# Mixture of experts by pairs of experts, its first groups prepared inside attention

## The chip, the cores and the metric

One core of a Trainium2 chip runs the whole kernel in one launch. The metric is the device time in microseconds, the median of several runs. TensorE (PE) multiplies, VectorE (DVE), ScalarE (ACT) and GpSimd (POOL) do element work, SyncE (SP) issues transfers and transposes by DMA. Each engine works through its own list in order and waits on semaphores.

## The reference

A vision tower of one layer over 64 images of 3x224x224. Each image gives 196 patches of 768 numbers and a class token, so 197 tokens of 192 channels:

```
h = concat(cls, patches @ W_lin.T + b_lin)            # 64 x 197 x 192
h = h + attention(layernorm(h))                        # 12 heads of 16, q and k normalised
x = layernorm(h)
h = h + moe(x)
moe(x):  s = sigmoid(x @ gate.T)                       # 8 experts in 4 groups
         biased = s + bias; best 2 of 4 groups by sum; best 2 experts in them
         w = s[chosen] / (sum + 1e-6)
         y = sum_e w_e * (silu(x @ w1_e.T) * (x @ w3_e.T)) @ w2_e.T
         z = same with the shared expert's weights, weight 1
```

All experts are computed for all tokens; the weight of those not chosen is 0. fp32 operands are split into two fp16 parts (hi and lo), so that a product is made of several fp16 matmuls.

## The kernel before

**Phase A** (`phase_a`, one block) does patches and attention. Its steps run as a pipeline over `k = 0 .. 68`: in step k, image k is embedded, k-2 is projected to q, k and v, k-3 is scored, k-4 attended, k-5 projected, added to the residual and stored to `hidden_dram`. Every engine has its own `step(k)` with the order of its work written out by hand. After step 63 no new image enters and the steps empty out.

**Phase B** (`phase_b`, a second block, which starts when all engines have left the first) takes the 12608 tokens from `hidden_dram` in 25 groups: 24 of 512 tokens (4 to a partition) and a last one of 320. For each group: SP loads `hin` (L994), DVE takes statistics (`stats_of`, L1171), POOL makes scale and shift (`rstds`, L1320 to L1329), ACT normalises and rounds to fp16 (`normalise`, L1108 to L1117), POOL takes the rest (`rest_of`, L1344), SP turns both parts by eight DMA transposes (L1008, L1009), PE multiplies by the gate (`gate`, 20 small matmuls, L1040), ACT takes tanh (L1123), and DVE picks the experts in 19 small steps cut into parts 0 to 5 (`route`). This is done one or two groups ahead, except for group 0 (and the normalising of group 1), which nothing precedes.

Nine experts (the ninth is the shared one) are computed for each group. For expert e:

- PE `inner_products`: eight matmuls of 128 rows (L1054 to L1057), then two "tails" of 64 rows (L1061), which use the upper and the lower half of the array beside each other, into the banks `ps_h1[b]` and `ps_h3[b]`, b alternating.
- ACT `silu` (L1132), DVE `multiply` (L1252), ACT `inner_first` (in_hi, L1140), POOL `inner_rest` (in_lo, L1337).
- PE `outer_products` (twelve matmuls, L1075 to L1077) for the expert two before, into `ps_y[0]` and `ps_y[1]`.
- DVE `accumulate` (L1270, or L1276 for the shared expert).

PE's order is inner(e), outer(e-2), inner(e+1), outer(e-1) and so on. POOL's `inner_rest(e)` also waits for the silu of expert e+1 (L1335), so that it starts when DVE starts the next multiply. An inner(e) waits for the multiply of e-2, an outer for the accumulation of the expert before, half by half.

Of the kernel before, what the change touches and what calls it, by code (L numbers as in the profile page):

```python
# [16 lines left out]
F32 = mybir.dt.float32  # L17
# [14 lines left out]
C = 192  # L32
# [73 lines left out]
def vit_layer(nc, xp, w_lin, bias_cls, w_qkv, w_proj, w_gate, gate_bias, w13, w2,  # L106
              ident, before4, before8, out):
    hidden_dram = nc.dram_tensor("hidden_dram", [IMAGES, TOKENS, C], F32).ap()
    with ExitStack() as ctx:
# [7 lines left out]
        with ExitStack() as passing:  # L117
# [23 lines left out]

            lin_f = stage("lin_f", [128, PCHUNKS, C])
# [39 lines left out]
            phase_a(nc, xp, hidden_dram, sem, locals())  # L182
        phase_b(nc, hidden_dram, out, sem, sb, locals())


def phase_a(nc, xp, hidden_dram, sem, bufs):
# [17 lines left out]
    with ExitStack() as ctx:  # L204
# [57 lines left out]

        def run(step):

            for k in range(IMAGES + 5):
                step(Index(0, k))
# [5 lines left out]
        def _(sp):  # L272
# [45 lines left out]
        def _(pe):  # L318
# [186 lines left out]
            run(step)  # L505


        @block.scalar
        def _(act):
# [90 lines left out]
            def step(k):  # L600
# [34 lines left out]
                if 0 <= k.c - FIRST_PIECE < PIECES:  # L635
                    mixture_piece(k.c - FIRST_PIECE)

# [4 lines left out]
            run(step)  # L642


        @block.vector
        def _(dve):
# [158 lines left out]
            def step(k):  # L805
# [42 lines left out]
                if k.c == 0:  # L848
                    attention_weights()

# [8 lines left out]
        def _(pool):  # L859
# [29 lines left out]
            for k in range(3, IMAGES + 3):  # L889
# [3 lines left out]
                strips_of(Index(0, k - 3), 1)  # L893


def phase_b(nc, hidden_dram, out, sem, sb, bufs):

    w13_hi, w13_lo, w2_hi, w2_lo, gate_hi, gate_lo, gbias, bef4, bef8, minus_half = (
        bufs[n] for n in "w13_hi w13_lo w2_hi w2_lo gate_hi gate_lo gbias bef4 bef8 minus_half".split())
    with ExitStack() as ctx:
        def ps(name, shape, dt=F32):
            return ctx.enter_context(nc.psum_tensor(name, shape, dt))

        T, E, G = LANES, EXPERTS, EGROUPS
        hin = [sb(f"hin{p}", [128, T, C]) for p in range(3)]
        acc = [sb(f"acc{p}", [128, T, C]) for p in range(2)]
# [9 lines left out]
        yT_lo = [sb(f"yT_lo{p}", [128, 2, GT], F16) for p in range(3)]  # L919
        act1 = [sb(f"act1{p}", [INTER, GT]) for p in range(2)]  # L920
        inner = [sb(f"inner{p}", [INTER, GT]) for p in range(3)]
        in_hi = [sb(f"in_hi{p}", [INTER, GT], F16) for p in range(3)]
        in_lo = [sb(f"in_lo{p}", [INTER, GT], F16) for p in range(3)]
        half = sb("half", [128, T, E])
# [19 lines left out]
        ps_y = [ps(f"ps_y{b}", [128, 512]) for b in range(2)]  # L944
        ps_gate = ps("ps_gate", [128, 512])

        h_in = [sem(f"h_in{p}") for p in range(3)]
        yT_in = [sem(f"yT_in{p}") for p in range(3)]
        acc_out = [sem(f"acc_out{p}") for p in range(2)]

        gate_done, inner_done, y_done = sem("gate_done"), sem("inner_done"), sem("y_done")

        yhi_done, tanh_done, silu_done, inhi_done = (
            sem("yhi_done"), sem("tanh_done"), sem("silu_done"), sem("inhi_done"))

        bst_done, bmv_done, bnorm_done, ylo_done = (
            sem("bst_done"), sem("bmv_done"), sem("bnorm_done"), sem("ylo_done"))
        route_step, route_done = sem("route_step"), sem("route_done")
        mul_done, inlo_done, acc_done = sem("mul_done"), sem("inlo_done"), sem("acc_done")

        bve_done, brstd_done, bshift_done, bneg_done = (
            sem("bve_done"), sem("brstd_done"), sem("bshift_done"), sem("bneg_done"))

        tokens_in = hidden_dram.rearrange("n t c -> (n t) c")
        tokens_out = out.rearrange("n t c -> (n t) c")
        LAST = FULL
        GROUPS_B = FULL + 1

        def rows_of(g):
            return REST if g.known and g.i * 2 + g.c == LAST else 128  # L970

        def full(dram):
            return dram[0:FULL * GT].rearrange("(g p t) c -> g p t c", p=128, t=T)

        def part(dram, g):
            if rows_of(g) == 128:
                return full(dram)[g.times(1)]
            return dram[FULL * GT:TOTAL].rearrange("(p t) c -> p t c", t=T)
# [9 lines left out]
        def _(sp):  # L988
            def load(g):
                p = g.mod(3)  # L990

                if reached(g.times(2 * NE, 2 - 6 * NE)):
                    sp.wait_ge(acc_done, g.times(2 * NE, 2 - 6 * NE))
                sp.dma_start(hin[p][0:rows_of(g)], part(tokens_in, g)).then_inc(h_in[p], 16)  # L994

# [5 lines left out]
            def transposes(g, half_no):  # L1001
                R, p = rows_of(g), g.mod(3)
                sp.wait_ge(ylo_done, g.times(2, half_no + 1))
                if half_no == 0 and reached(g.times(NE, -2 * NE)):
                    sp.wait_ge(inner_done, g.times(NE, -2 * NE))
                for t in (2 * half_no, 2 * half_no + 1):
                    s = slice(t * R, (t + 1) * R)
                    sp.dma_start_transpose(yT_hi[p][:, :, s], y_hi[0:R, t, :]).then_inc(yT_in[p], 16)  # L1008
                    sp.dma_start_transpose(yT_lo[p][:, :, s], y_lo[0:R, t, :]).then_inc(yT_in[p], 16)  # L1009

            for g in range(3):
                load(Index(0, g, 2, GROUPS_B))
            for g in range(2):
                transposes(Index(0, g, 2, GROUPS_B), 0)
                transposes(Index(0, g, 2, GROUPS_B), 1)

            def body(g):
                ahead = g.back(-2)
                if g.back(-3).active():
                    load(g.back(-3))  # L1020
                if ahead.active():
                    transposes(ahead, 0)
                    transposes(ahead, 1)
# [6 lines left out]
        def _(pe):  # L1030
            def gate(g):
                R, p = rows_of(g), g.mod(3)
                pe.wait_ge(yT_in[p], 32 * T * (g.c // 3 + 1))

                if reached(g.times(1)):
                    pe.wait_ge(tanh_done, g.times(1))
                for t in range(T):
                    s = slice(t * R, (t + 1) * R)
                    dst = ps_gate[0:R, t * E:(t + 1) * E]
                    pe.matmul(dst, yT_hi[p][:, 0, s], gate_hi[:, 0], start=True, stop=False)  # L1040
                    pe.matmul(dst, yT_hi[p][:, 0, s], gate_lo[:, 0], start=False, stop=False)
                    pe.matmul(dst, yT_lo[p][:, 0, s], gate_hi[:, 0], start=False, stop=False)
                    pe.matmul(dst, yT_hi[p][:, 1, s], gate_hi[:, 1], start=False, stop=False)
                    last = pe.matmul(dst, yT_lo[p][:, 1, s], gate_lo[:, 1], start=False, stop=True)
                last.then_inc(gate_done, 1)

            def inner_products(g, e):
# [5 lines left out]
                for w, bank in enumerate(banks):  # L1053
# [3 lines left out]
                    pe.matmul(bank, w13_hi[:, 1, e, w, :], y_hi[:, 1], start=False, stop=False)  # L1057
                for w, bank in enumerate(banks):
# [5 lines left out]
            def outer_products(g, e):  # L1064
                R, b = rows_of(g), e % 3
# [351 lines left out]
```

## Time and profile before

| | us |
|---|---|
| median of 3 runs | 1692.89 (1692.03 to 1693.24) |
| the profiled execution, device time | 1693.34 |
| its span, first to last instruction | 1690.9 |
| PE busy in the span | 1602.8 (95%) |
| DVE, ACT, POOL busy | 1276.7, 989.0, 676.4 |
| mean granted TensorE clock, share of full | 0.985 |

The profiled execution is 0.45 us above the median. PE's busy time is made of modelled spans of overlapping matmuls, so start-to-start distances in the timeline say more than durations.

### The profile page before, as it was taken

How to read it: one execution, taken by the hardware profiler on the slowest of the kernel's cores; microseconds unless marked ns; L12 is line 12 of the kernel's file. 1: busy time of each engine (PE TensorE's matmuls, PEld its weight loads, DVE VectorE, ACT ScalarE, POOL GpSimd, SP SyncE). 2: the span in 40 equal slices, each digit the busy share in tenths (PEclk: the TensorE clock that was granted, in tenths of full speed). 3: DMA queues.
4: the chain of work that ended last, by engine and by line, in shares of the span. 5: the costliest groups of instructions: out<-in, count | busy, mean ns of one | idle time of the engine just before them, and what ended most of it. 6: DMA issues, size and time to landing. Idle time of an engine off the chain costs nothing. (4 is left out here: it accounts for less than half of the span.)

```text
span 1690.9 us, 44146 instructions
## 1 busy us (share of the span) xinstructions
PE 1602.8 (95%) x16714; PEld 1098.8 (65%) x16714; DVE 1276.7 (76%) x3610; ACT 989.0 (58%) x2039; POOL 676.4 (40%) x758
## 2 busy tenths in 40 slices
PE   4999999999999999999998299999999999999998
PEld 4777777777777777777776155555555555555555
DVE  5777877777777777777774288888887888888877
ACT  2777777667777777777676245454545454444543
POOL 2333333333333333333331255454554545454543
PEclk8999999999999999999999599999999999999999
DMA  7233333333333333333310211212121111112110
GB/s 245 64 78 78 77 77 78 77 78 78 80 79 79 79 82 80 78 81 78 77 27 12 56 47 37 59 34 61 33 58 38 45 51 43 53 40 56 34 36 16
DMA packets 97695, 108.11 MB, mean 64 GB/s; under 512 B 61323, under 2 KB 74286, under 8 KB 97358
## 3 DMA queue, kind: packets, MB, share of 16 engines
q1 hardware_dynamic: 88270, 85.83, 17.6%
q0 software_dynamic: 9216, 19.47, 7.6%
q8 instruction: 134, 2.20, 0.5%
q14 instruction: 75, 0.61, 0.1%
HBM read 92.44 MB, written 19.37 MB: 66 GB/s over the span
## 5 line engine op out<-in xcount | busy, mean ns | idle before, releaser
L1337 POOL TENSOR_TENSOR in_lo<-inner,in_hi 128x512 f16<-128x512 f32 (+1 forms) x225 | 259.7, 1154 | 347.8 <-ACT act L1132 335.4
L884 POOL CAST qk_strips<-qk_norm 99x768 f16<-99x768 f32 x128 | 105.2, 822 | 583.1 <-DVE qk_norm L753 583.1
L589 ACT ACTIVATE prob<-ps_sc 99x792 f32<-99x792 f32 x384 | 303.8, 828 | 6.2 <-PE ps_sc L404 2.6
L1140 ACT ACTIVATE in_hi<-inner 128x512 f16<-128x512 f32 (+1 forms) x225 | 140.3, 623 | 203.5 <-DVE inner L1252 203.5
L1270 DVE SCALAR_TENSOR_TENSOR acc<-ps_y,comb,acc 128x192 f32<-128x192 f32 (+1 forms) x700 | 242.0, 408 | 0.3 <-PE ps_y L1077 0.3
L1132 ACT ACTIVATE act<-ps_h 128x512 f32<-128x512 f32 (+1 forms) x225 | 131.9, 586 | 168.4 <-PE ps_h L1061 168.4
L1252 DVE SCALAR_TENSOR_TENSOR inner<-ps_h,act 128x512 f32<-128x512 f32 (+1 forms) x225 | 153.0, 680 | 102.3 <-ACT act L1132 99.9
L1075 PE MATMUL ps_y<-w_hi,in_hi 128*128 128x192 f16 (+1 forms) x900 | 224.2, 249 | 4.0 <-DVE acc L1270 3.4
L1077 PE MATMUL ps_y<-w_hi,in_lo 128*128 128x192 f16 (+1 forms) x900 | 221.4, 246 | 0.0
L1076 PE MATMUL ps_y<-w_lo,in_hi 128*128 128x192 f16 (+1 forms) x900 | 221.4, 246 | 0.0
L342 PE MATMUL ps_hid<-lin_hi,x_hi 128*99 128x192 f16 x768 | 193.9, 252 | 19.1 <-DVE x_lo L701 10.4
L344 PE MATMUL ps_hid<-lin_hi,x_lo 128*99 128x192 f16 x768 | 190.9, 249 | 0.0
L343 PE MATMUL ps_hid<-lin_lo,x_hi 128*99 128x192 f16 x768 | 190.9, 249 | 0.0
L1054 PE MATMUL ps_h<-yT_hi,w_hi 128*128 128x512 f16 (+1 forms) x450 | 169.5, 377 | 1.9 <-DVE inner L1252 1.9
L886 POOL TENSOR_TENSOR qk_strips<-qk_norm,qk_strips 99x384 f16<-99x384 f32 x128 | 165.9, 1296 | 10.6
L419 PE MATMUL ps_o<-prob,v 98*32 98x198 f32 (+1 forms) x3072 | 169.8, 338 | 0.0
L1057 PE MATMUL ps_h<-yT_hi,w_hi 128*128 128x512 f16 (+1 forms) x450 | 169.6, 377 | 0.0
L1056 PE MATMUL ps_h<-yT_hi,w_lo 128*128 128x512 f16 (+1 forms) x450 | 169.6, 377 | 0.0
L1055 PE MATMUL ps_h<-yT_lo,w_hi 128*128 128x512 f16 (+1 forms) x450 | 169.6, 377 | 0.0
L764 DVE COPY kT<-ps_mix 128x594 f16<-128x594 f16 x128 | 60.5, 473 | 96.9 <-PE ps_mix L388 96.2
L571 ACT ACTIVATE qT<-ps_mix 128x594 f16<-128x594 f16 x128 | 86.8, 678 | 66.8 <-PE ps_mix L388 66.8
L404 PE MATMUL ps_sc<-qT,kT 64*99 64x198 f16 x1536 | 105.8, 256 | 21.1 <-ACT prob L589 19.9
(157 smaller groups left out, 3807.3 us busy)
## 6 DMA issues: line engine op xcount, KB each, us to landing
xin<-xp SPq DMA_DIRECT2D x64, 594.0 KB, 4.3
x_hi<-xp POOLq DMA_DIRECT2D x64, 297.0 KB, 4.1
hidden_dram<-h SPq DMA_DIRECT2D x64, 147.0 KB
hin<-hidden_dram SPq DMA_DIRECT2D x24, 384.0 KB, 3.5
out<-acc SPq DMA_DIRECT2D x24, 384.0 KB, 2.7
w_f<-w SPq DMA_DIRECT2D x1, 2304.0 KB, 9.1
yT_hi<-y_hi SPq DMA_TRANSPOSE x100, 2.4
yT_lo<-y_lo SPq DMA_TRANSPOSE x100, 2.4
```

Source lines behind the costliest of these rows:

```text
L342: pe.matmul(hid[:, t, :], hi[:, k, s], lin_hi[:, k, :], start=(k == 0), stop=False)
L343: pe.matmul(hid[:, t, :], hi[:, k, s], lin_lo[:, k, :], start=False, stop=False)
L344: last = pe.matmul(hid[:, t, :], lo[:, k, s], lin_hi[:, k, :], start=False, stop=(k == PCHUNKS - 1))
L419: last = pe.matmul(o_quad[VB * place:VB * place + VB, :], v[p][rows, m, QUAD * quad + place, :], prob[quad][rows, place, m, :], start=(m = ...
L589: act.activation(prob[quad][:, places].rearrange("p h m s -> p h (m s)"), ps_sc[0:TR, places, 0:2 * SLOTS], ACT.Exp, scale=D ** -0.5 / (SQ ...
L1055: pe.matmul(bank, w13_hi[:, 0, e, w, :], y_lo[:, 0], start=False, stop=False)
L1056: pe.matmul(bank, w13_lo[:, 0, e, w, :], y_hi[:, 0], start=False, stop=False)
L1075: pe.matmul(dst, in_hi[b][:, s], w2_hi[:, e, :], start=True, stop=False)
L1076: pe.matmul(dst, in_hi[b][:, s], w2_lo[:, e, :], start=False, stop=False)
L1077: last = pe.matmul(dst, in_lo[b][:, s], w2_hi[:, e, :], start=False, stop=True)
L1270: last = dve.scalar_tensor_tensor(out=acc[p][0:R, t, :], in0=ps_y[half_no][0:R, u * C:(u + 1) * C], scalar=comb[p][0:R, t, e:e + 1], in1=b ...
L1337: pool.tensor_tensor(in_lo[b][:, 0:N], inner[b][:, 0:N], in_hi[b][:, 0:N], ALU.subtract).then_inc(inlo_done, 1)
```

## The change

Two edits. First, the objects for preparing a group's rows move out of `phase_b` into a class `MixtureRows` that lives through both phases, and phase A's steps call it. SP loads groups 0 to 2 in step 58. DVE takes group 0's statistics at the end of steps 61 and 62 and group 1's at the end of steps 66 and 67. POOL makes group 0's scale and shift after its step 63. ACT normalises group 0 at the end of steps 64 and 65, POOL takes the rest in steps 65 and 66, SP issues four transposes in each of its steps 65 and 66 after the store. ACT loads the table for silu at the end of step 67. After its last step PE multiplies group 0 by the gate (into the unused end of `ps_hid`), ACT normalises group 1 and takes group 0's tanh, and POOL makes group 1's scale, shift and rest. Group 1's eight transposes are SP's first work in phase B.

Second, experts are done two at a time over the whole run of 225 (group, expert) pairs. The buffers `inner`, `in_hi`, `in_lo` go from 3 to 4, `ps_y` from 2 banks to 4 (a pair for each parity of the expert); the gate's scores go to the end of one of them. POOL's wait for the next silu is gone.

```
+                if k.c == IMAGES - 6:                      # SP, phase A
+                    for p in range(2):
+                        sp.wait_ge(h2_out[p], 32 * 4)
+                    for g in range(3):
+                        rows.load(sp, b_group(g))
+                if k.c in (IMAGES + 1, IMAGES + 2):
+                    rows.transposes(sp, b_group(0), k.c - IMAGES - 1)
             run(step)                                      # PE, phase A
+            pe.wait_ge(v_set, IMAGES)
+            rows.gate(pe, b_group(0), ps_gate)
+                if k.c in (IMAGES, IMAGES + 1):            # ACT, phase A
+                    rows.normalise(act, b_group(0), k.c - IMAGES)
+                if k.c == IMAGES + 3:
+                    act.preload_act_table_set("silu_and_others")
             run(step)
+            rows.normalise(act, b_group(1), 0)
+            rows.normalise(act, b_group(1), 1)
+            rows.gate_out(act, b_group(0), ps_gate)
+                if k.c in (IMAGES - 3, IMAGES - 2):        # DVE, phase A
+                    rows.stats_of(dve, b_group(0), k.c - IMAGES + 3)
+                if k.c in (IMAGES + 2, IMAGES + 3):
+                    if k.c == IMAGES + 2:
+                        dve.wait_ge(rows.bneg_done, 1)
+                    rows.stats_of(dve, b_group(1), k.c - IMAGES - 2)
+                if k == IMAGES - 1:                        # POOL, phase A
+                    rows.rstds(pool, b_group(0))
+                if k in (IMAGES + 1, IMAGES + 2):
+                    rows.rest_of(pool, b_group(0), k - IMAGES - 1)
+            rows.rstds(pool, b_group(1))
+            rows.rest_of(pool, b_group(1), 0)
+            rows.rest_of(pool, b_group(1), 1)
...
+        def two_by_two(own_work, older_work):              # phase B
+            turns = [(Index(0, g, 2, GROUPS_B), e) for g in range(GROUPS_B) for e in range(NE)]
+            for i in range(0, len(turns) + 2, 2):
+                own, older = turns[i:i + 2], turns[max(i - 2, 0):i]
+                own_work(own, lambda: [older_work(g, e) for g, e in older])
...
             def outer_products(g, e):
-                R, b = rows_of(g), e % 3
+                if g.c == 0 and e == 0:
+                    pe.wait_ge(tanh_done, 1)
+                R, b, y = rows_of(g), (NE * g.c + e) % 4, ps_y[(g.c + e) % 2]
...
-                    if reached(g.times(2 * NE, 2 * e + half_no - 1)):
-                        pe.wait_ge(acc_done, g.times(2 * NE, 2 * e + half_no - 1))
+                    if reached(g.times(2 * NE, 2 * e + half_no - 3)):
+                        pe.wait_ge(acc_done, g.times(2 * NE, 2 * e + half_no - 3))
...
+            def turn(own, older_products):                 # PE
+                for g, e in own:
                     inner_products(g, e)
+                scored = [g.back(-1) for g, e in own if e == 3 and g.back(-1).active()]
+                for following in scored:
+                    g, e = own[0]
+                    if reached(g.times(2 * NE, 2 * e - 6)):
+                        pe.wait_ge(acc_done, g.times(2 * NE, 2 * e - 6))
+                    rows.gate(pe, following, ps_gate)
+                for g, e in own:
+                    inner_tails(g, e)
+                for following in scored:
+                    pe.wait_ge(tanh_done, following.times(1, 1))
+                older_products()
+            two_by_two(turn, outer_products)
...
+            def turn(own, _):                              # ACT
+                for g, e in own:
+                    if e == 3 and g.back(-1).active():
+                        if g.c == 0:
+                            act.wait_ge(route_step, 1)
+                        rows.gate_out(act, g.back(-1), ps_gate)
+                for g, e in own:
                     silu(g, e)
+                for g, e in own:
                     inner_first(g, e)
+                for g, e in own:
+                    ahead = g.back(-2)
+                    if e == 5 and ahead.active():
+                        rows.normalise(act, ahead, 0)
+                    if e == 6 + g.c % 2 and ahead.active():
+                        rows.normalise(act, ahead, 1)
...
+            def turn(own, older_sums):                     # DVE
+                for g, e in own:
                     multiply(g, e)
+                older_sums()
+                for g, e in own:
+                    following, ahead = g.back(-1), g.back(-2)
+                    if g.c == 0 and e == 0:
+                        for part_no in range(5):
+                            route(g, part_no)
+                    if e == 0:
+                        route(g, 5)
                     if e in (1, 2) and ahead.active():
+                        rows.stats_of(dve, ahead, e - 1)
+                    if e > 3 and following.active():
                         route(following, e - 4)
...
             def inner_rest(g, e):                          # POOL
                 pool.wait_ge(inhi_done, g.times(NE, e + 1))
-                if e + 1 < NE or g.back(-1).active():
-                    pool.wait_ge(silu_done, g.times(NE, e + 2))
...
                     if e == 3 and g.back(-2).active():
+                        rows.rstds(pool, g.back(-2))
+                    if e == 6 and g.back(-2).active():
+                        rows.rest_of(pool, g.back(-2), 0)
+                    if e == 7 + g.c % 2 and g.back(-2).active():
+                        rows.rest_of(pool, g.back(-2), 1)
```

`inner_tails` is the second half of the old `inner_products` (the two matmuls of 64 rows), unchanged; the methods of `MixtureRows` are the old local functions with the engine as an argument.

## Rows read from the trace of the kernel before

**Rows 1.** Stretches: busy us (instructions) by engine, TensorE clock, DMA share, GB/s.
```profile
937.00:963.50 26.50, 0.51 (x19) 0.51 (x20) 3.66 (x17) 4.76 (x12) 5.96 (x12) 0.50 0.25 71
1000.00:1640.00 640.00, 639.08 (x4828) 366.18 (x4827) 533.36 (x1617) 311.78 (x597) 326.96 (x375) 1.00 0.18 46
```

**Rows 2.** Waits of PE from 970 us on: us in total, times, longest.
```profile
PE ps_y L1075 <- DVE acc L1270: 3.4, 6, 1.1
```

**Rows 3.** Timeline between the phases: start, us, engine, line, operation, idle before it.
```profile
936.86 0.56 DVE L802 SCALAR_TENSOR_TENSOR h<-ps_mix,h 99x384 f32<-99x384 f32 x1 [1.99 <-PE ps_mix L325]
...
940.31 1.29 SPq L994 DMA_DIRECT2D hin<-hidden_dram  x3
...
948.37 0.98 ACT L1108 ACTIVATE bnorm<-hin,bshift,brstd 128x192 f32<-128x192 f32 x2 [14.11 <-POOL bshift L1329]
...
950.01 0.97 ACT L1108 ACTIVATE bnorm<-hin,bshift,brstd 128x192 f32<-128x192 f32 x2
...
951.51 1.29 SPq L1008 DMA_TRANSPOSE yT_hi<-y_hi  x1
...
960.56 1.25 SPq L1009 DMA_TRANSPOSE yT_lo<-y_lo  x1
...
962.99 0.19 PE L1040 MATMUL ps_gate<-gate_hi,yT_hi 128*128 128x8 f16 x1 [26.17 <-DMA yT_lo<-y_lo]
...
963.55 0.59 PE L1054 MATMUL ps_h<-yT_hi,w_hi 128*128 128x512 f16 x1
```

**Rows 4.** Timeline of PE in the mixture, one expert's worth.
```profile
1302.98 0.38 PE L1054 MATMUL ps_h<-yT_hi,w_hi 128*128 128x512 f16 x1
...
1304.49 0.38 PE L1057 MATMUL ps_h<-yT_hi,w_hi 128*128 128x512 f16 x1
...
1304.80 0.39 PE L1061 MATMUL ps_h<-yT_lo,w_lo 64*128 64x512 f16 x2
...
1305.13 0.26 PE L1075 MATMUL ps_y<-w_hi,in_hi 128*128 128x192 f16 x1
...
1306.13 0.38 PE L1054 MATMUL ps_h<-yT_hi,w_hi 128*128 128x512 f16 x1
```

**Rows 5.** Timeline of group 0: route parts 2 and 3, multiply, next inner.
```profile
968.74 0.17 DVE L1223 TENSOR_SCALAR chosen<-rank 128x16 f32<-128x16 f32 x1
...
970.86 0.69 DVE L1252 SCALAR_TENSOR_TENSOR inner<-ps_h,act 128x512 f32<-128x512 f32 x1
...
971.61 0.39 PE L1054 MATMUL ps_h<-yT_hi,w_hi 128*128 128x512 f16 x1 [1.86 <-DVE inner L1252]
```

**Rows 6.** Timeline of PE in attention: four successive couples of 64-row matmuls.
```profile
797.52 0.55 PE L404 MATMUL ps_sc<-qT,kT 64*99 64x198 f16 x8
...
797.82 0.25 PE L404 MATMUL ps_sc<-qT,kT 64*99 64x198 f16 x2
```

**Rows 7.** The tanh's line (duration ns min/median/max, first and last start).
```profile
L1123 ACT ACTIVATE half<-ps_gate x25: 175/178/198, 966.7 to 1644.4; 128x32 f32<-128x32 f32 x24, 80x32 f32<-80x32 f32 x1
```

**Rows 8.** Timeline of the mixture, what follows the tails that start at 1301.66.
```profile
1302.09 0.60 ACT L1132 ACTIVATE act<-ps_h 128x512 f32<-128x512 f32 x1 [1.16 <-PE ps_h L1061]
...
1302.78 0.69 DVE L1252 SCALAR_TENSOR_TENSOR inner<-ps_h,act 128x512 f32<-128x512 f32 x1 [0.69 <-ACT act L1132]
...
1303.39 1.38 DVE L1270 SCALAR_TENSOR_TENSOR acc<-ps_y,comb,acc 128x192 f32<-128x192 f32 x4
...
1303.51 0.63 ACT L1140 ACTIVATE in_hi<-inner 128x512 f16<-128x512 f32 x1 [0.82 <-DVE inner L1252]
```

**Rows 9.** One line of part 3 (duration ns min/median/max).
```profile
L1198 DVE TENSOR_TENSOR cmp<-masked x23: 411/615/919, 1025.0 to 1661.5; 128x256 f32<-128x256 f32 x22, 80x256 f32<-80x256 f32 x1
```

**Rows 10.** Timeline of POOL and DVE at 1575 us.
```profile
1575.32 1.16 POOL L1337 TENSOR_TENSOR in_lo<-inner,in_hi 128x512 f16<-128x512 f32 x1 [0.25 <-issue]
...
1575.38 1.37 DVE L1200 TENSOR_TENSOR eq<-eq,bef 128x256 f32<-128x256 f32 x1
```

**Rows 11.** Timeline of POOL, a rest of the rows ahead.
```profile
1573.58 0.92 POOL L1344 TENSOR_TENSOR y_lo<-bnorm,y_hi 128x384 f16<-128x384 f32 x1
```

More of the change, by code:

```diff
@@ new lines, in gate_out @@
+        def gate_out(act, g, bank):
+            R = rows_of(g)
+            act.wait_ge(gate_done, g.times(1, 1))
+            act.activation(half[0:R], bank[0:R, 0:T * E].rearrange("p (t e) -> p t e", e=E), ACT.Tanh,
+                           scale=0.5 / SS).then_inc(tanh_done, 1)
+        self.hin = hin
+        self.y_hi = y_hi
+        self.y_lo = y_lo
+        self.yT_hi = yT_hi
+        self.yT_lo = yT_lo
+        self.yT_in = yT_in
+        self.inner_done = inner_done
+        self.acc_done = acc_done
@@ new lines, in __init__, with phase_b, ps @@
+        self.bneg_done = bneg_done
+        self.rows_of = rows_of
+        self.part = part
+        self.tokens_out = tokens_out
+        self.GROUPS_B = GROUPS_B
+        self.half, self.gate_done, self.tanh_done = half, gate_done, tanh_done
+        self.gate, self.gate_out = gate, gate_out
+        self.load = load
+        self.transposes = transposes
+        self.normalise = normalise
+        self.stats_of = stats_of
+        self.rstds = rstds
+        self.rest_of = rest_of
+def phase_b(nc, out, sem, sb, rows, bufs):
+    w13_hi, w13_lo, w2_hi, w2_lo, gate_hi, gate_lo, gbias, bef4, bef8, minus_half = (
+        bufs[n] for n in "w13_hi w13_lo w2_hi w2_lo gate_hi gate_lo gbias bef4 bef8 minus_half".split())
+    hin, y_hi, y_lo, yT_hi, yT_lo, yT_in, inner_done, acc_done, rows_of, part, tokens_out, GROUPS_B = (
+        rows.hin, rows.y_hi, rows.y_lo, rows.yT_hi, rows.yT_lo, rows.yT_in, rows.inner_done, rows.acc_done, rows.rows_of, rows.part, rows.tokens_out, rows.GROUPS_B)
+    with ExitStack() as ctx:
+        def ps(name, shape, dt=F32):
+            return ctx.enter_context(nc.psum_tensor(name, shape, dt))
+        T, E, G = LANES, EXPERTS, EGROUPS
+        acc = [sb(f"acc{p}", [128, T, C]) for p in range(2)]
@@ L920, in phase_b @@
         act1 = [sb(f"act1{p}", [INTER, GT]) for p in range(2)]
[L921 to L924, printed above, removed]
+        inner = [sb(f"inner{p}", [INTER, GT]) for p in range(4)]
+        in_hi = [sb(f"in_hi{p}", [INTER, GT], F16) for p in range(4)]
+        in_lo = [sb(f"in_lo{p}", [INTER, GT], F16) for p in range(4)]
@@ L999, in store @@
                 sp.dma_start(part(tokens_out, g), acc[p][0:rows_of(g)]).then_inc(acc_out[p], 16)
[L1001 to L1015, printed above, removed]
+            second = Index(0, 1, 2, GROUPS_B)
+            rows.transposes(sp, second, 0)
+            rows.transposes(sp, second, 1)
             def body(g):
@@ L1019, in body @@
                 if g.back(-3).active():
-                    load(g.back(-3))
+                    rows.load(sp, g.back(-3))
                 if ahead.active():
-                    transposes(ahead, 0)
-                    transposes(ahead, 1)
+                    rows.transposes(sp, ahead, 0)
+                    rows.transposes(sp, ahead, 1)
                 store(g)
@@ L1030, in _ @@
         def _(pe):
[L1031 to L1045, printed above, removed]
             def inner_products(g, e):
```

300 lines of the change are left out of this document (131 added, 169 removed).

## The prediction, made blind

> **What bounds the kernel now.** I read the busy times by stretches first. In the mixture, from 1000 to 1640 us, PE is busy 639.1 of 640 us at full clock and DVE 533.4 [rows 1]; in the stretch from 937 to 963.5 us PE does 0.5 us of work in 26.5 and its clock is granted at 0.50, the lower of its two levels (1.2 GHz) [rows 1]. So there are two places to gain: the gap between the phases, and PE's own time in the mixture, where only work or lost slots of PE count. The waits confirm it: from 970 us to the end PE waits 3.4 us for DVE's sums, in six places [rows 2], and for little else.
>
> The timeline shows what the gap is made of [rows 3]: the last residual ends at 937.4, the first load is issued at 940.31 (store landed, engines in the new block), group 0's normalising can start at 948.37, its eight transposes go out from 951.51 to 960.56, one per 1.29 us, the last lands 2.43 us after its issue, and PE starts at 962.99 with the gate (0.56 us) and at 963.55 with the experts.
>
> One expert on PE takes 1306.13 - 1302.98 = 3.15 us [rows 4]. Eight full matmuls start 1.51/7 = 0.215 us apart. The tails start 0.31 after the last of them, and the first outer matmul 0.33 after the tails; at the pace of 512 columns each would be 0.215. So 0.095 + 0.11 = 0.205 us are lost around each couple of tails. The twelve outer matmuls take 1.00.
>
> **The change part by part.**
>
> *The gap.* Loading, statistics, scale and shift, normalising, eight transposes and gate of group 0 leave the gap. What they displace in attention: DVE's statistics (four short instructions a half, 1.2 us by the 0.30 an instruction below) fall at the ends of steps in which its loads shrink; I count nothing. ACT's normalise takes 950.01 - 948.37 = 1.64 us a half [rows 3] and stands in front of step 65's and step 66's exponents and copies, which the shortened steps wait for one after another. Bounds 0 and 3.3 us; I take 2, since the first stands before the copy that projection waits for and the second meets some slack. SP's eight transposes take its queue for 4 x 1.29 = 5.2 us twice, behind stores 60 and 61; images follow each other some 14 us apart (68 steps to 937), so the next store waits for nothing. The first tanh's table load is hidden in step 67, where ACT idles. So attention ends at 939.4, and the new block starts 2.9 us behind it as now (940.31 - 937.4), at 942.3. Behind this hides group 1's chain: ACT's last copy lies some 3 us before the last residual's end (a correction, the projection and the residual are between), at 936.4; two halves of 1.64 go to 939.7, the tanh to 940.2, POOL's last rest (two operations, 0.92 [rows 11] and, with a third of the columns, some 0.4, an estimate) to 941.2. They end about with the store; I set PE's first expert at 943.0. It is 962.99 now: **-20.0**. Group 0's gate, 0.56, is done beside ACT: **-0.5**.
>
> *The start of the mixture.* Now, at 971.61 PE starts its third expert [rows 5], having done 0.56 + 2 x 3.15 - 2 x 1.00 = 4.9 us of work in 8.6: 3.7 lost. After: half clock at first loses some 2 (both); nothing older covers the first silu and multiply, 1.3; group 1's eight transposes start only at 943 and land at 943 + 9.05 + 2.43 = 954.5, where PE asks for them at about 954, 0.7; DVE does route parts 0 to 5 between the second and the third multiply, 22 instructions at 2.12/7 = 0.30 [rows 5], 6.7 us, and a half of statistics: 1.2. Together 5.2: **+1.5**. At nought to +4.
>
> *Pairs on PE.* 112 times two experts: one stay of tails instead of two. Saved 0.205 each, if the second couple of tails follows the first at 0.215. The nearest rows: four couples of 64-row matmuls in attention start within 0.30 us, 0.10 apart for 198 columns [rows 6], which is 0.08 of streaming. So loading the next 64-row weights hides under the running ones but for 0.02. Bounds per pair: 0.205 and 0.10 (no hiding, one 0.10 load each); I take 0.20: 112 x 0.20 = **-22.4**.
>
> *Four banks of ps_y.* DVE's sums may now be a turn late; the 3.4 us of rows 2 go, but the tail of the run keeps some: **-2**.
>
> *The gate turns.* PE now waits for the tanh between tails and outer products. Gate matmuls, then 0.65 us of tails; tanh takes 0.18 [rows 7], with hand-overs 0.45. Hidden: 0. The 25 tanh share the table with silu today (one load each at the start only), so no reloads.
>
> *The new tight place.* Let a pair's tails start at 0. Now tails at 1301.66 (one period before 1304.80) are followed by silu at +0.43, multiply at +1.12 [rows 8], and PE can use the bank 971.61 - 970.86 = 0.75 after a multiply starts [rows 5]: +1.87. With pairs PE asks for it after the second tails (0.215), the change back (0.325) and 24 outer matmuls (1.98), at +2.52. So DVE may come 0.65 us late to a pair's first multiply; beyond that PE stands. Before, it asked a whole expert later. The turn is 2 x 3.15 - 0.2 = 6.1 us, DVE's work in it two multiplies (0.61 each, 1303.39 - 1302.78) and two sums (1.38 each less an overlap of 0.08 with what follows), which is 3.8, and routing or statistics. Parts 2 and 3 together take 970.86 - 968.74 = 2.1 us [rows 5], the largest load: 5.9, under 6.1. So DVE alone is never late.
>
> But DVE and POOL hold each other up. The compare of part 3 takes 0.41 alone and up to 0.92, median 0.62 [rows 9]; at 1575.38 the next operation of that size takes 1.37 beside POOL's in_lo of 1575.32 and ends 0.3 after it [rows 10]. Sums and multiplies (one operand in PSUM) take their usual time beside in_lo [rows 8]. With in_hi at +1.85 for 0.63 [rows 8] and the wait for the next silu gone, the two in_lo of a pair (1.16 each) run from about +2.7 to +4.9, beside the sums: free. The rests of the rows ahead (0.92 and some 0.4) come where routing is. In even groups experts 6 and 7 share a turn: POOL does in_lo, rest, in_lo, rest without a break from +2.7 to +7.4; DVE comes at +4.9 with parts 2 and 3, is held 0.8 behind in_lo, 0.9 and 0.4 behind the rest, and ends at +9.0 instead of +7.0. The next multiply was due at +7.2: 1.8 late, PE stands 1.2. In odd groups the rests fall after both in_lo in the turns (5,6) and (7,8), beside parts 1 to 4: by the same count 0.3 and 1.0. Upper bound 12 x 1.2 + 11 x 1.3 = 29; lower bound 0, if POOL and DVE slip past each other. I take the first in full and a third of the second: **+19**.
>
> A rule speaks here. The Trainium skill, page "SBUF — State Buffer", section "SBUF: two separate sides", says that DVE operations with two SBUF inputs and GpSimd operations exclude each other for a whole instruction, whoever starts first. By it alone each meeting costs the rest of POOL's instruction, and the sum would take the upper bound, 29; by the median of the compare a meeting costs 0.2, five of them 1.0 a turn, and almost nothing would reach PE. The trace agrees with the rule in its maxima (0.92, 1.37).
>
> **Sum**, against the profiled 1693.34: -20.0 - 0.5 + 1.5 - 22.4 - 2 + 19 = -24.4, so 1668.9; the median of the runs is 0.45 lower: **1668**.
>
> **The rivals.**
>
> *A. The contention stays hidden* (0.35). DVE and POOL miss each other, or ACT's normalise pushes the rest later, past the routing. For it: DVE has 5.4 us of work a turn on average (533.4 us in 100 turns' time), so lateness is made good at once. Against: POOL's work in turn (6,7) has no break. Then -43: 1649.
>
> *B. Weights of the second tails are not loaded beside the first* (0.07). Each pair saves 0.10 only: 11 us less, 1679. The couples in attention speak against it.
>
> *C. The handover gains little* (0.05). Something at phase A's end (group 1's rest, DVE behind transposes) holds the block's end some 12 us: 1680. Against: the estimate of every chain ends by 941.3.
>
> *D. Slower: DVE bound* (0.04). If DVE is held in every turn as in turn (6,7), by 2.0 us, a turn lasts 5.4 + 2.0 = 7.4 instead of the 6.3 of today: 112 x 1.1 = 123 more, less the 19 of the gap: 1797. It decides from 1.05 us of holding per turn on (5.4 + 1.05 = 6.3 + 19/112). Against it: rests fall in two or three turns of nine, and in the others POOL is done by +4.9.
>
> *The forecast, part of the contention shows*, has 0.49. Its own range is 1657 to 1681.
>
> The range for 8 in 10: from just under A with its uncertainties (a shorter gap, 1645) to above B and C, 1684. A difference under 0.2% (3.4 us) can't be told from none: faster needs less than 1689.5. All of forecast, A, B and C are faster, less a tail of the forecast: 0.93 faster, 0.03 same, 0.04 slower.
>
> **What would show it.** PE's first expert starts near 943 instead of 963.55, its clock low for some 4 us. One pair of experts takes 6.1 us between first inner matmuls, with one stretch of four tails, the second couple 0.21 to 0.23 after the first. The table of waits shows PE's first full matmul of a pair (L1054 now) waiting for DVE's multiply (some 1 to 1.3 us, once or twice in two groups) and hardly for its sums; those waits follow turns with experts 6 and 7 (5 and 6, 7 and 8), where DVE's compares run to 0.9 us and more. If that wait is missing, A holds. If the distance of the couples is over 0.3, B. If PE starts after 950, C. If a turn lasts over 6.3 on average, D, and I am wrong in sign.

## The result, and the profile after

The changed kernel takes **1680.75 us** (median of 3, 1680.17 to 1683.59) against 1692.89: 0.9934 times the time before, 95% interval 0.9915 to 0.9954. The profiled execution has a span of 1678.2 us against 1690.9. So it is faster by 12.1 us, a little under half of the forecast 24.9 (1692.89 to 1668), and inside the range. The sign held, and PE does stand for late multiplies as forecast; several terms of the sum had the wrong size.

The stretches of the changed kernel, columns as in [rows 1]:

```profile
937.00:963.50 26.50, 15.16 (x113) 8.03 (x111) 10.08 (x30) 6.00 (x14) 4.86 (x6) 0.74 0.12 26
1000.00:1640.00 640.00, 618.92 (x4796) 366.17 (x4795) 565.32 (x1598) 303.69 (x594) 319.50 (x374) 1.00 0.17 45
```

PE works 15.2 us in the gap's 26.5, where it did 0.5 [rows 1]. But in the mixture, where it was busy for 639.1 of 640 us, it is now busy for 618.9: 20 us of standing are new. PE's waits from 970 us on name what it stands for (us in total, times, longest):

```profile
PE ps_h L1191 <- DVE inner L1357: 19.7, 25, 1.0
PE ps_y L1056 <- issue: 2.8, 11, 0.5
PE ps_y L1219 <- POOL in_lo L1411: 0.4, 1, 0.4
```

The waits for sums of [rows 2] are gone. In their place PE waits 25 times for DVE's multiply before a pair's first matmul, and 11 times before the gate (the view puts these down to "issue"; what they are is read further below).

Counted from the starts of PE's matmuls, a turn of two experts takes 6.08 us bare (two single ones took 2 x 3.143), and the nine turns of two groups take on average 6.94, 6.98, 6.08, 6.08, 7.19, 6.09, 6.59, 6.08 and 6.19, beginning with experts (0,1) of the even group. The gate's 0.5 is in the second and the seventh. So PE loses 0.86 before turn (2,3), 1.11 after turn (8,0), 0.11 after the odd group's turn (7,8), and 0.42 in the even group's gate turn. DVE does a turn's multiplies first and its routing last, so each of these losses is the lateness left by the routing one turn earlier: 0.86 by the odd group's turn (7,8), 1.11 by turn (6,7), 0.11 by turn (5,6).

The totals by stage, in the profiled execution of each kernel (us; the same count; "rest" runs from the first expert of the last group to the end of the span):

| kernel | last residual starts | first expert | first two groups | two groups, mean of the next 22 | rest |
|---|---|---|---|---|---|
| before | 936.86 | 963.55 | 59.90 | 57.85 | 31.1 |
| changed | 938.38 | 946.33 | 63.29 | 58.21 | 28.2 |
| rows' part alone (x1) | 942.92 | 950.88 | 57.80 | 57.78 | 31.1 |
| pairs alone (x2) | 936.90 | 963.15 | 62.10 | 58.30 | 28.2 |
| remainders beside the multiplies (x3) | 940.40 | 948.36 | 61.85 | 55.72 | 28.2 |
| rows earlier (x4) | 940.72 | 943.98 | 62.28 | 58.23 | 28.2 |
| routing first (x6) | 938.24 | 946.19 | 58.73 | 58.18 | 28.2 |
| x3, x4 (earlier still) and x6 (x9) | 937.19 | 940.46 | 57.81 | 55.69 | 28.2 |

Where the mixture loses, the timeline of POOL and DVE in an even group's turn (6,7) shows (start, us, engine, line, operation):

```profile
1036.87 0.91 POOL L1043 TENSOR_TENSOR y_lo<-bnorm,y_hi 128x384 f16<-128x384 f32 x1
1037.75 0.42 POOL L1044 TENSOR_TENSOR y_lo<-bnorm,y_hi 128x128 f16<-128x128 f32 x1
1038.13 1.15 POOL L1411 TENSOR_TENSOR in_lo<-inner,in_hi 128x512 f16<-128x512 f32 x1
1038.15 1.16 DVE L1328 TENSOR_SCALAR chosen<-rank 128x16 f32<-128x16 f32 x1
1039.25 0.91 POOL L1043 TENSOR_TENSOR y_lo<-bnorm,y_hi 128x384 f16<-128x384 f32 x1
1039.35 0.84 DVE L1330 TENSOR_SCALAR drop<-chosen 128x16 f32<-128x16 f32 x1
1040.12 0.42 POOL L1044 TENSOR_TENSOR y_lo<-bnorm,y_hi 128x128 f16<-128x128 f32 x1
1040.22 0.37 DVE L1334 TENSOR_TENSOR masked<-biased,chosen 128x32 f32<-128x32 f32 x1
...
1042.10 1.29 DVE L1357 SCALAR_TENSOR_TENSOR inner<-ps_h,act 128x512 f32<-128x512 f32 x2
```

Read the ends: chosen ends at 1039.31, POOL's in_lo at 1039.28; drop at 1040.19, POOL's first subtraction at 1040.16; masked at 1040.59, the second at 1040.54. Each DVE instruction, of 0.17 to 0.19 us by itself, lasts until POOL's is over, three times in a row, 1.8 us in all. The multiply starts at 1042.10, and PE, due at 1041.7, starts at 1042.85.

### The profile page after: what moved, and what is told of

Its sections match the earlier page's. It is cut to its first block and busy times, and to the rows that moved or that the text cites. A ratio compares the mean times of both kernels' runs of the same rounds, so it can differ in the third digit from the quotient of the medians.

```text
span 1678.2 us, 44142 instructions
## 1 busy us (share of the span) xinstructions
PE 1586.3 (95%) x16714; PEld 1102.9 (66%) x16714; DVE 1315.0 (78%) x3610; ACT 978.6 (58%) x2038; POOL 669.8 (40%) x758
## 5 line engine op out<-in xcount | busy, mean ns | idle before, releaser
L1411 POOL TENSOR_TENSOR in_lo<-inner,in_hi 128x512 f16<-128x512 f32 (+1 forms) x225 | 253.6, 1144 | 353.6 <-ACT in_hi L1258 353.5
L1250 ACT ACTIVATE act<-ps_h 128x512 f32<-128x512 f32 (+1 forms) x225 | 120.7, 588 | 224.8 <-PE ps_h L1203 221.7
L1191 PE MATMUL ps_h<-yT_hi,w_hi 128*128 128x512 f16 (+1 forms) x450 | 170.7, 379 | 31.1 <-DVE inner L1357 23.6
L1357 DVE SCALAR_TENSOR_TENSOR inner<-ps_h,act 128x512 f32<-128x512 f32 (+1 forms) x225 | 143.1, 678 | 71.3 <-ACT act L1250 53.8
L1258 ACT ACTIVATE in_hi<-inner 128x512 f16<-128x512 f32 (+1 forms) x225 | 136.5, 624 | 91.8 <-DVE inner L1357 91.8
```

The source lines that it names most:

```text
L1191: pe.matmul(bank, w13_hi[:, 0, e, w, :], y_hi[:, 0], start=True, stop=False)
L1411: pool.tensor_tensor(in_lo[b][:, 0:N], inner[b][:, 0:N], in_hi[b][:, 0:N], ALU.subtract).then_inc(inlo_done, 1)
```

## The experiments

**The two parts, each alone.** x1 keeps the rows' part and takes back the order of before; x2 keeps the pairs and takes back the rows' part.

```diff
-        ps_y = [[ps(f"ps_y{b}{half_no}", [128, 512]) for half_no in range(2)] for b in range(2)]
-        ps_gate = ps_y[0][1][:, 2 * C:512]
+        ps_y = [ps(f"ps_y{b}", [128, 512]) for b in range(2)]
+        ps_gate = ps("ps_gate", [128, 512])
...
-            two_by_two(turn, outer_products)
+            run(body)
...
```

Every engine's loop of the mixture is that of before again. x2, at the mixture's start and likewise on each engine:

```diff
-                if k.c in (IMAGES, IMAGES + 1):
-                    rows.normalise(act, b_group(0), k.c - IMAGES)
...
+            for c in range(2):
+                rows.normalise(act, Index(0, c, 2, GROUPS_B), 0)
+                rows.normalise(act, Index(0, c, 2, GROUPS_B), 1)
```

> The rows' part alone: the first two groups' rows are prepared in the last steps of attention as in the changed kernel, but the mixture keeps the order of before, one expert after the other, with three inner buffers and two ps_y banks. Theory (the earlier start is all that the change has won, and the pairs lose a little): TensorE's first expert starts at about 946, as after the change, two groups of the mixture take 57.9 us as before, and the whole takes 1674 to 1678, some 4 us less than the changed kernel. Rival (the pairs win too, and the earlier start is given back in the mixture's first turns): two groups again take 57.9 us, but the time is 1681 or more.

x1: 1675.39 us, ratio 0.9902 (0.9888 to 0.9915), faster than the change as a whole, with 57.8 us for two groups. Its first expert started at 950.88, not at about 946: attention itself ended 4.5 us later in the profiled execution, though its code is that of the changed kernel (more on this at the end of the next section).

> The pairs alone: the mixture's order of the changed kernel, the rows prepared after attention as before. Theory (each turn saves 0.2 us on TensorE, and the turns' stalls take more than that back): two groups take 58.2 us against 57.87 of before, and the whole 1692 to 1697, no faster than before. Rival (the pairs by themselves are worth their 22 us and only collide with the handover's work): 1670 to 1676, two groups in 56 us.

x2: 1696.21 us, ratio 1.0022 (1.0013 to 1.0031), two groups in 58.3. So all the gain is the rows' part, and the pairs, as placed, cost about 4 us by themselves and 5 beside the rows' part. Counted from the first expert on they cost 7.3 there ((63.29 - 57.80) + 11 x (58.21 - 57.78) + 28.2 - 31.1); part of it hides in x1's later end of attention. The rivals fall.

**What the stalls of the pairs are.**

```diff
                 for e in range(NE):
+                    if e in (6 - g.c % 2, 8 - g.c % 2) and g.back(-2).active():
+                        pool.wait_ge(silu_done, g.times(NE, e + 1))
+                        rows.rest_of(pool, g.back(-2), int(e > 6))
                     inner_rest(g, e)
-                    if e == 3 and g.back(-2).active():
+                    if e == 3 - g.c % 2 and g.back(-2).active():
                         rows.rstds(pool, g.back(-2))
-                    if e == 6 and g.back(-2).active():
-                        rows.rest_of(pool, g.back(-2), 0)
-                    if e == 7 + g.c % 2 and g.back(-2).active():
-                        rows.rest_of(pool, g.back(-2), 1)
...
-                    if e == 6 + g.c % 2 and ahead.active():
+                    if e == 6 - g.c % 2 and ahead.active():
                         rows.normalise(act, ahead, 1)
```

(The first half's normalising likewise: e == 5 - g.c % 2.)

> The changed kernel with one thing placed otherwise: GpSimd's remainders of the rows (y_lo) wait for the next turn's first silu, so that they run beside VectorE's two multiplies, which read PSUM, and not beside its routing; in odd groups the normalising and the remainders come a turn earlier, so that their transposes land before the gate. Theory 1 (GpSimd's remainders hold VectorE's routing instructions, whose lateness stalls TensorE 0.85 and 1.1 us in two of nine turns, and the odd groups' transposes land 0.3 us late for the gate): the chosen and drop instructions fall from 1.16 and 0.84 us to under 0.3, both stalls fall under 0.4 us, two groups take 56.0 to 56.8 us against 58.22, the whole 1657 to 1665. Rival (these two turns simply hold too much VectorE work, with or without GpSimd beside it): the holds go, the stalls stay near 0.7 and 0.9, two groups take 57.7 or more, the whole 1674 or more.

x3: **1654.41 us**, ratio 0.9774 (0.9760 to 0.9787), 26 us under the changed kernel. Its rows: PE's waits, the stretch of [rows 1], the two held lines (ns min/median/max) and one turn; ahead of them the two held lines of the changed kernel:

```profile
L1328 DVE TENSOR_SCALAR chosen<-rank x21: 166/176/1166, 1038.2 to 1620.4; 128x16 f32<-128x16 f32 x21
L1330 DVE TENSOR_SCALAR drop<-chosen x21: 174/835/1007, 1039.3 to 1620.6; 128x16 f32<-128x16 f32 x21
```

```profile
PE ps_h L1191 <- DVE inner L1357: 0.6, 2, 0.4
...
1000.00:1640.00 640.00, 639.43 (x5026) 387.14 (x5026) 552.18 (x1670) 311.76 (x611) 326.87 (x381) 1.00 0.17 45
...
L1328 DVE TENSOR_SCALAR chosen<-rank x22: 161/168/174, 1037.5 to 1620.7; 128x16 f32<-128x16 f32 x21, 80x16 f32<-80x16 f32 x1
L1330 DVE TENSOR_SCALAR drop<-chosen x22: 171/174/175, 1037.7 to 1620.9; 128x16 f32<-128x16 f32 x21, 80x16 f32<-80x16 f32 x1
...
1039.65 0.91 POOL L1043 TENSOR_TENSOR y_lo<-bnorm,y_hi 128x384 f16<-128x384 f32 x1 [2.26 <-ACT act L1250]
1039.67 1.29 DVE L1357 SCALAR_TENSOR_TENSOR inner<-ps_h,act 128x512 f32<-128x512 f32 x2
1040.52 0.42 POOL L1044 TENSOR_TENSOR y_lo<-bnorm,y_hi 128x128 f16<-128x128 f32 x1
```

The same subtractions run beside two multiplies, which read one operand from PSUM and keep their 1.29 us. DVE does the same routing in the same turns, and PE waits 0.6 us in all instead of 19.7. So the rival, too much DVE work in these turns, falls. The stalls were the holds. All nine turns are bare but for the gate, 55.72 us for two groups, less than I had expected (56.0 to 56.8), and so is the whole (1657 to 1665 expected). One reservation: x3 also moves the odd groups' rows a turn earlier, so by itself it does not part the holds from the late transposes. In even groups only the place of the remainders changed, and the 1.11 after turn (8,0) is gone. The gate turn, where the odd groups' transposes count, went from 6.98 to 6.56, so 11 x 0.42 = 4.6 of the 26 us are theirs. The next rows show that wait.

In the changed kernel the odd groups' last remainder ends at 1014.12, the last transpose goes out at 1017.93, and the gate stands until it has landed, at 1020.27:

```profile
1013.51 0.61 POOL L1044 TENSOR_TENSOR y_lo<-bnorm,y_hi 128x128 f16<-128x128 f32 x1
...
1017.93 1.25 SPq L991 DMA_TRANSPOSE yT_lo<-y_lo  x1
...
1020.37 0.17 PE L1056 MATMUL ps_y<-gate_hi,yT_hi 128*128 128x8 f16 x1 [0.18 <-issue]
```

The view puts only 0.18 of it down, to "issue". The PE queue's own record of this wait, for the transposes and for the tanh of the group before, runs from 1017.17 to 1020.31, and the matmul before it would have let the gate start at 1020.02.

**What holds the handover.** Each engine's list for a block ends in an instruction DRAIN, called its closing drain here. The blocks' end in the changed kernel:

```profile
939.32 0.29 SPq L293 DMA_DIRECT2D hidden_dram<-h  x1
939.44 0.91 POOL L1043 TENSOR_TENSOR y_lo<-bnorm,y_hi 128x384 f16<-128x384 f32 x1 [0.33 <-ACT y_hi L1010]
940.31 0.43 POOL L1044 TENSOR_TENSOR y_lo<-bnorm,y_hi 128x128 f16<-128x128 f32 x1
946.30 1.17 SPq L990 DMA_TRANSPOSE yT_hi<-y_hi  x1
...
946.33 0.59 PE L1191 MATMUL ps_h<-yT_hi,w_hi 128*128 128x512 f16 x1 [7.47 <-PEq L206]
```

Nothing computes or moves from 941.4 to 946.3. The trace's record of GpSimd's closing drain runs from 939.41 to 946.05, 5.3 us past its last subtraction (940.73), while SP had closed at 941.43. Before, that drain lay at 911.8 to 918.1, hidden. x4 moves the rows' work three attention steps earlier:

```diff
-                if k.c in (IMAGES, IMAGES + 1):
-                    rows.normalise(act, b_group(0), k.c - IMAGES)
+                if k.c in (IMAGES - 3, IMAGES - 2):
+                    rows.normalise(act, b_group(0), k.c - IMAGES + 3)
+                if k.c in (IMAGES, IMAGES + 1):
+                    rows.normalise(act, b_group(1), k.c - IMAGES)
...
-            rows.normalise(act, b_group(1), 0)
-            rows.normalise(act, b_group(1), 1)
```

Loads, statistics, remainders and transposes of both groups go with it.

> The changed kernel with the rows' work three steps of attention earlier, and group 1's transposes inside attention too, so that GpSimd's last instruction of attention ends near 915 instead of 940.7. Theory (the mixture's first expert waits for GpSimd's closing drain, which ends 5 to 6 us after its last instruction, 946.05 in the changed kernel; without it the last store decides): first expert at 940.5 to 942.5, the whole 3 to 5 us less than the changed kernel, 1676 to 1678. Rival 1 (the handover is bound by something else of the same length, such as the last store or the fetch of the new code): first expert stays at 945 to 947, 1680 to 1682. Rival 2 (the work taken into full steps of attention delays each of them): attention's last residual comes 2 to 5 us later than 938.4, and the gain is gone.

x4: 1676.99 us, ratio 0.9906 (0.9892 to 0.9920). First expert 3.26 us behind the last residual's start instead of 7.95. GpSimd's last instruction ended at 919.63, not near 915, and its drain at 924.95, still out of the way. Rows of x4:

```profile
941.65 0.29 SPq L293 DMA_DIRECT2D hidden_dram<-h  x1
...
943.98 0.58 PE L1188 MATMUL ps_h<-yT_hi,w_hi 128*128 128x512 f16 x1 [2.78 <-PEq L206]
```

The expert did not start at 940.5 to 942.5, since the residual itself came 2.3 us later, as rival 2 had it; most of that is one step at a lower clock (below). The time's interval overlaps that of the changed kernel (0.9915 to 0.9954), so what x4 shows is in the trace, not in the 3.8 us of the medians. x4 moves much else; x5 touches the drain alone, it is the kernel before with one instruction more:

```diff
+            pool.wait_ge(h2_done, IMAGES)
+            pool.memset(eps[:], EPS)
```

> The kernel before with one instruction more: GpSimd clears one column ([128 x 1]) once attention's last residual is done, and has nothing else to do there. Theory (GpSimd's closing drain ends 5 to 6 us after its last instruction, whatever that is, and the mixture's block waits for it): the drain that ended at 918.1 in the kernel before ends at 943 to 944, SyncE's first load of the mixture goes out at 943.2 to 944.3 instead of 940.31, and the whole takes 1695 to 1697. Rival (the 5.3 us behind the last instruction came from what GpSimd had to do there, two long subtractions, or overlapped something else): the first load stays within 0.7 us of 940.31 and the time at 1692 to 1693.5.

x5: 1696.08 us (one run, before 1692.75). Its rows:

```profile
938.00 0.10 POOL L895 MEMSET eps<- 128x1 f32 x1 [24.73 <-DVE h L802]
938.31 0.29 SPq L286 DMA_DIRECT2D hidden_dram<-h  x1
943.64 1.29 SPq L996 DMA_DIRECT2D hin<-hidden_dram  x3
```

The first load goes out at 943.64, not 940.31 [rows 3]; the drain ends at 943.39, again 5.3 us behind a 0.1 us instruction. Of the 3.3 us, 0.5 are the residual's own (937.38 against 936.86). The theory holds. What makes the drain so long is open: the mixture's own takes 0.9. x10 tried one cause:

```diff
+            pool.dma_start(scratch[:], tokens_in[0:128]).then_inc(scratch_in, 16)
+            pool.wait_ge(scratch_in, 16)
```

> The kernel before with one DMA more that GpSimd issues and waits for at the start of the mixture, 128 rows of 768 B into a tile that nothing reads. In the kernel before GpSimd issues 64 DMAs in attention and none in the mixture, and its closing drain ends 5.3 us after its last instruction in the one and at most 0.9 us in the other. Theory (the drain is long in a stretch of the program in which GpSimd has issued a DMA): the mixture's closing drain grows from 0.88 us to some 5 us or more. Rival (its length has to do with attention's other work or with the new code behind it): it stays at 0.9 us. The time hardly tells them apart: 1692 to 1697 in both, since the last store ends 7 us after GpSimd's last instruction.

The mixture's drain takes 0.97 us, as the rival has it: one early DMA of GpSimd does not make it long. (1690.95 us, one run.)

**The first turns.**

```diff
-                    if g.c == 0 and e == 0:
-                        for part_no in range(5):
-                            route(g, part_no)
...
+            for part_no in range(5):
+                route(Index(0, 0, 2, GROUPS_B), part_no)
```

> The changed kernel with group 0's routing (parts 0 to 4) at the start of VectorE's mixture work, where it idles until the first silu, instead of behind the first two multiplies. Theory (TensorE's waits of 1.2 and 2.7 us before the second and third turns come from VectorE being late, the third's from this routing): the third turn starts 2.3 to 3 us after 963.65 less, that is at 960.7 to 961.5, and the whole takes 1676.5 to 1679. Rival (the first turns are held by the low clock and by the transposes of group 1, which land at 957.3, so that a wait that goes is replaced by another): the third turn at 963 or later, 1680 to 1682.

x6: 1675.12 us, ratio 0.9903 (0.9887 to 0.9920). The third turn starts 3.0 us earlier and without a wait (first row the changed kernel, second x6), and the turn after it loses nothing either, where it had lost 1.7: 4.6 us in the first two groups. The time is 1.4 us under what I expected, since only the third turn's wait was counted.

```profile
963.65 0.39 PE L1191 MATMUL ps_h<-yT_hi,w_hi 128*128 128x512 f16 x1 [2.69 <-DVE inner L1357]
```

```profile
960.64 0.38 PE L1191 MATMUL ps_h<-yT_hi,w_hi 128*128 128x512 f16 x1
```

**All of it.** x9 joins x3 and x6 and moves the rows a further three steps forward, so that none of their work is left in attention's last, shortened steps.

```diff
-                if k.c == IMAGES - 6:
+                if k.c == IMAGES - 12:
                     for p in range(2):
                         sp.wait_ge(h2_out[p], 32 * 4)
...
-                if k.c in (IMAGES, IMAGES + 1):
-                    rows.normalise(act, b_group(0), k.c - IMAGES)
+                if k.c in (IMAGES - 6, IMAGES - 5):
+                    rows.normalise(act, b_group(0), k.c - IMAGES + 6)
+                if k.c in (IMAGES - 3, IMAGES - 2):
+                    rows.normalise(act, b_group(1), k.c - IMAGES + 3)
```

> All remedies together: GpSimd's remainders beside the multiplies, group 0's routing first, and both groups' rows and transposes done in full steps of attention, six and more steps before its end, so that nothing of them is left in the last, shortened steps. Theory (the costs found are separate and add): attention's last residual at 937 to 938.5, first expert 3.3 us later at 940.3 to 941.8, first turns 3 us shorter, two groups in 55.7 us, the whole 1640 to 1646. Rival 1 (the last steps of attention still lose 2 to 4 us to a lower granted clock, with or without the rows' work in them): last residual at 940 or later, 1645 to 1650. Rival 2 (the first turns' waits turn into others): 1648 to 1653.

x9: **1641.02 us** (1640.65 to 1641.10), ratio 0.9696 (0.9682 to 0.9710), with attention's end, the first expert and two groups where the theory has them. The first two groups are 5.5 us shorter than in the changed kernel instead of 3 (63.29 to 57.81).

```profile
940.46 0.59 PE L1188 MATMUL ps_h<-yT_hi,w_hi 128*128 128x512 f16 x1 [2.79 <-PEq L206]
...
1000.00:1620.00 620.00, 619.58 (x4869) 374.40 (x4868) 535.15 (x1621) 302.90 (x592) 316.91 (x369) 1.00 0.17 46
```

## Why the prediction was wrong

In the prediction's own terms (us; measured from the starts of PE's matmuls, twelve pairs of groups):

| term | predicted | measured |
|---|---|---|
| gap and gate | -20.5 | 946.33 - 963.55 = -17.2 |
| start of the mixture | +1.5 | (63.29 - 58.21) - (59.90 - 57.85) = +3.0 |
| pairs | -22.4 | 12 x 9 x (6.287 - 6.077) = -22.7, and 0.9 in the last group = -23.6 |
| four banks | -2 | 12 x 0.26, and 2.0 in the last group = -5 |
| gate turns | 0 | 12 x 0.42 = +5 |
| contention | +19 | 12 x (1.11 + 0.86 + 0.11) = +25 |
| sum | -24.4 | -13 (the two profiled spans differ by 12.8) |

- *The pairs on PE* came out as counted: what is lost around the tails is paid once instead of twice, and the second couple of tails starts 0.226 us after the first (median of 113), so loading its weights costs next to nothing. Rival B is out.
- *The four banks* gave 3 us more than counted: of PE's waits for DVE's sums, 2.8 us lay in the last group, and none is left. That it made up for part of the misses below is luck.
- *The contention* is the largest miss, and the step that failed is "a third of the second". Turn (6,7) was counted at 1.2 and costs 1.11. The odd groups' turns were counted at 0.3 and 1.0 and cost 0.11 and 0.86, nearly the full count. The prediction gives no reason for the third; the low price that it names beside it is the median of the compare [rows 9], 0.2 us over 0.41. The trace of the kernel before shows what lies behind a compare of just that length:

```profile
1053.32 0.92 POOL L1344 TENSOR_TENSOR y_lo<-bnorm,y_hi 128x384 f16<-128x384 f32 x1
...
1053.90 0.61 DVE L1198 TENSOR_TENSOR cmp<-masked 128x256 f32<-128x256 f32 x1
```

The compare starts when POOL's subtraction has 0.34 us left, and ends 0.27 after it. So the 0.2 is the price of a meeting that began late in POOL's instruction, and not a low price per meeting. In the changed kernel chosen and drop start with POOL's instructions, and pay nearly all of them (1038.15 beside 1038.13, 1039.35 beside 1039.25). (Whether the wait for the next silu, which the change removes, had kept these meetings late was not tested by itself.) The rule quoted in the prediction (the Trainium skill, "SBUF — State Buffer", "SBUF: two separate sides") was the better guide, +29 by its bound; the same section also counts VectorE's two-port modes among what excludes GpSimd, and the trace shows chosen and drop, with one SBUF input each, taking 1.16 and 0.84.
- *The gate turns* were set to 0 with an eye on the tanh alone. That wait does cost nothing (tails to outer products take 0.54 us with and without a gate). The step that failed is "Hidden: 0", which leaves out the wait before the gate: the second remainder of an odd group's rows stands at expert 8, so its four transposes, one per 1.3 us on SP, land 0.3 us late for the next gate.
- *The gap*: attention's delay (2 counted, 1.5 measured) and POOL's last rest (941.2 counted, 940.7 measured) are right. The step that failed is "they end about with the store", the move from the last instruction to the block's end. For POOL this takes 5.3 us, so the first expert starts at 946.3 and not at 943.0. Without it, at the 3.3 us behind the last residual's start of x4 and x9, it would have started at 941.7. Rival C named the place, but not the price.
- *The start*: the one-off routing between the multiplies was seen; it took 7.7 us (954.39 to 962.1; two instructions of 0.2 took 1.1 each beside POOL's in_lo) instead of 6.7. PE waited 1.2 us for DVE before the second turn and 2.7 before the third, and the turn after that was 1.7 longer than bare. x6 shows that 4.6 us of this need not be there.
- *Rival D* reckons with 5.4 us of VectorE work a turn. 533.4 us [rows 1] in 640 / 6.29 turns are 5.2. Nothing in the result hangs on it.

Not foreseen either: x1, x3 and x4 lose another 3 to 4 us in one step of attention (16.5 to 17.7 us between two residuals; 13.7 in the profiles of the changed kernel and x6, 12.7 before). x1, x3, x6 and the changed kernel have the same code there. The rows of 900 to 905 and 905 to 910, first of the changed kernel, then of x6, then of x1 (PE busy, granted clock, DMA):

```profile
900.00:905.00 5.00, 3.31 (x45) 1.00 0.02 3
905.00:910.00 5.00, 4.44 (x61) 1.00 0.00 0
```

```profile
900.00:905.00 5.00, 3.20 (x43) 1.00 0.01 3
905.00:910.00 5.00, 4.55 (x63) 1.00 0.00 0
```

```profile
900.00:905.00 5.00, 3.25 (x38) 0.91 0.00 0
905.00:910.00 5.00, 4.44 (x38) 0.50 0.02 3
```

With the normalising on ACT in this step, PE is idle for 1.7 to 1.8 us of the first five, where it was idle for 1.2 before. In x1, x3 and x4 the clock is then granted at its lower level, 0.50 (1.2 GHz), for 7 to 10 us; in the changed kernel and in x6 it is not. With the rows moved to full steps (x9) PE is busy 4.21 us there and the step takes 12.66 us at full clock. That the idle time causes the drop is argued from these traces, not tested by itself, and it is not enough alone, as x6 shows. The kernel before has such a difference too: from 916.2 to 923.0 us its clock is granted at 0.50, while x10, with the same attention code, keeps 1.00 up to 932.7, and the last three steps take 29.0 us in the one and 26.5 in the other. So 2 to 4 us of a single time can come from attention's clock alone, and the table by stage says more than the totals.

## What to carry to other kernels

When two engines hold each other up and a change shifts their work, count their meetings at full price in every period: from where the one instruction starts to where the other ends. Put what GpSimd subtracts beside VectorE's instructions that read PSUM: with the odd groups' rows a turn earlier, this was worth 26 us here, some 5 of them for the gate. Work moved into the end of a phase is free only if it also leaves the closing of each engine's block alone; look for the last instruction of each engine, and what lies between it and the first of the next phase. A chain that ends in a queue (remainder, transposes, gate) is traced to its last landing, not to the instruction one is thinking of.

## What the hardware showed unexpectedly

- GpSimd's closing drain ends 5.3 us after its last instruction in attention, behind a 0.43 us subtraction and behind a 0.10 us memset alike, and 0.1 to 0.2 us after it in the mixture (0.88 and 0.97 in all). The cause stayed open.
- VectorE's TENSOR_SCALAR with one small SBUF input (128x16, 0.17 us by itself) took up to 1.17 us beside GpSimd, and in the turn shown ended within 0.05 us of GpSimd's instruction. Multiplies and sums with an operand in PSUM are not held: two multiplies take 1.29 us beside GpSimd's subtractions and without them, and all 800 sums of the changed kernel last 0.40 to 0.42 us.
- The granted clock differs between executions of the same attention code: after 1.7 us of idle TensorE one step took 17.7 us at the lower level in x1 and 13.7 at full clock in the changed kernel.
